# Local attention in groups of two row steps

## The reference

```
def local_attention(q, k, v):            # (b, heads, n, 64)
    bq = q.reshape(b, h, w, WINDOW, d) * QK_SCALE          # WINDOW = 128
    bk, bv = look_around(bk), look_around(bv)              # the window before and its own
    sim = einsum('bhwid,bhwjd->bhwij', bq, bk)
    mask = (i < j) | (i > j + WINDOW) | (j == -1)
    attn = softmax(where(mask, -max, sim))
    return einsum('bhwij,bhwjd->bhwid', attn, bv)
```

## Time and profile before

| | |
|---|---|
| median of 3 runs | 7475.08 us |
| lowest and highest | 7471.83 and 7477.56 us |
| profiled execution: time, span | 7471.83 us, 7471.8 us |
| mean granted clock of TensorE | 0.921 |
| busy: PE, DVE, ACT, POOL | 83%, 63%, 37%, 18% of the span |
| first and last score product of the four stages | 1310.7 to 1529.7, 2135.5 to 2353.6, 6043.2 to 6262.9, 6871.9 to 7090.5 us |

### The profile page before, as it was taken

How to read it: one execution, slowest core, us unless ns; L and a number is a source line. 1 busy time by engine, 2 the same in 40 slices (tenths; PEclk the granted TensorE clock), 3 DMA queues, 4 the chain that set the end, 5 groups by cost and what they waited for, 6 DMA issues and landing times. The chain is left out here.

```text
span 7471.8 us, 109245 instructions
## 1 busy us (share of the span) xinstructions
PE 6232.5 (83%) x31152; PEld 3226.2 (43%) x31152; DVE 4699.7 (63%) x11759; ACT 2751.9 (37%) x6050; POOL 1321.0 (18%) x1051
## 2 busy tenths in 40 slices
PE   5788859989988886999974588987995888998979
PEld 2333334655456442222223353344553456544655
DVE  4666557734665545999967649984336764357735
ACT  0155514722354210666651105541110364224711
POOL 1211106100431002000000005530003531025100
PEclk9899979989999997999996699998998999999989
DMA  5433244652456435333314221124212456235541
GB/s 165 129 72 69 62 129 145 190 188 81 130 164 196 143 101 174 80 80 83 87 50 118 81 82 40 37 73 112 73 50 90 142 165 196 72 94 154 174 151 54
DMA packets 946481, 836.62 MB, mean 112 GB/s; under 512 B 240872, under 2 KB 801984, under 8 KB 945728
## 3 DMA queue, kind: packets, MB, share of 16 engines
q1 hardware_dynamic: 498352, 507.29, 23.5%
q10 hardware_dynamic: 425472, 304.20, 13.1%
q0 software_dynamic: 22144, 18.99, 0.8%
HBM read 506.25 MB, written 346.03 MB: 114 GB/s over the span
## 5 line engine op out<-in xcount | busy, mean ns | idle before, releaser
L1395 ACT ACTIVATE Catt_E<-Catt_t 128x512 f32<-128x512 f32 x1024 | 579.1, 596 | 321.1 <-DVE Catt_t L1358 246.8
L1344 DVE CUSTOM_DVE_ANT_0 Catt_S<-Catt_s,Catt_win 128x1024 f32<-128x1024 f32 x512 | 621.5, 1215 | 4.9 <-DMA Catt_win<-skewed 3.2
L1344 DVE CUSTOM_DVE_ANT_0 Aatt_S<-Aatt_s,Aatt_win 128x128 f32<-128x128 f32 (+7 forms) x512 | 379.2, 757 | 233.7 <-PE Aatt_s L1271 206.6
L1395 ACT ACTIVATE Aatt_E<-Aatt_t 128x512 f32<-128x512 f32 (+3 forms) x768 | 341.3, 491 | 251.3 <-PE Aatt_t L1303 201.8
L1300 PE MATMUL Catt_t<-Catt_Q,Catt_K 123*128 123x512 bf16 x1024 | 364.8, 388 | 46.9 <-ACT Catt_E L1395 19.6
L1271 PE MATMUL Catt_s<-Catt_K,Catt_Q 96*128 96x512 bf16 x1024 | 322.9, 398 | 22.3 <-DMA Catt_K<-k_parts 12.1
L1358 DVE TENSOR_TENSOR Catt_t<-Catt_t,Catt_near 128x256 f32<-128x256 f32 (+2 forms) x640 | 284.8, 457 | 85.7 <-PE Catt_t L1300 77.4
L1322 PE MATMUL Catt_o<-Catt_E,Catt_V 128*32 128x256 f32 x4096 | 327.0, 391 | 0.0
L2362 PE MATMUL scan_cum<-scan_X,scan_upto 128*128 128x512 f32 x512 | 264.7, 607 | 25.4 <-DVE scan_X L2431 23.7
L2360 PE MATMUL scan_cum<-scan_X,scan_after 128*128 128x512 f32 x448 | 240.6, 619 | 40.9 <-DVE scan_pi L2442 40.9
L1322 PE MATMUL Aatt_o<-Aatt_E,Aatt_V 128*32 128x256 f32 (+1 forms) x2816 | 222.9, 361 | 41.7 <-ACT Aatt_O L1403 41.6
(11 more groups left out here) (723 smaller groups left out, 14232.4 us busy)
## 6 DMA issues: line engine op xcount, KB each, us to landing
moe_cb<-c_s SPq DMA_DIRECT2D x16, 1024.0 KB
skewed<-lines POOLq DMA_DIRECT2D x8, 1920.0 KB, 12.8
Catt_win<-skewed SPq DMA_DIRECT2D x16, 960.0 KB, 4.7
rec<-state_in_r ACTq DMA_DIRECT2D x32, 416.0 KB
scan_r<-rec SPq DMA_DIRECT2D x64, 208.0 KB, 2.5
Aatt_Q<-q_parts SPq DMA_DIRECT2D x32, 384.0 KB, 4.3
Aatt_K<-k_parts SPq DMA_DIRECT2D x32, 384.0 KB, 5.6
Catt_Q<-q_parts SPq DMA_DIRECT2D x32, 384.0 KB, 4.3
```

What stands on the lines that cost most here:

```text
L1344: v.tensor_tensor_reduce(out=S[:, j % 2, 0:w], in0=s_ps[j % 2][:, 0:w], in1=win[:, 0 if causal else h, w0:w0 + w], scale=-1.0, scalar=BIG, ...
L1395: a.activation(E[:, kb % NB, h, lo:hi], bank(it, n)[:, 0:hi - lo], ACT.Exp, scale=scale).then_inc(exped, 1)
```

## The change

Row steps go by groups of two: group i is steps 2i and 2i+1. TensorE does, at position i, the scores of group i (four products with one wait before them and one semaphore increment behind the last), the turns of group i-2, the values of group i-3, and `turn_sums` last. One bank `s_ps[i % 2][h]` holds both steps' scores of head h, in its first and its second half. VectorE waits once for all scores of a group, then does its four masks; its copies have a lag of two groups. ScalarE does `move_o` (lag 4) first, then the exponentials of the first step, the copy, and those of the second. The rings S, E and `nmax` have 8 slots instead of 4, and the counts of the semaphores follow.

```diff
@@ -769,8 +769,9 @@
 
 def stage_local_attention(nc, name, q_s, k_s, v_s, r_s, oT_s, scale):
 
-    PAIRS, hd, R, PT_R = 4, 64, 4, 4
+    PAIRS, hd, R, PT_R = 4, 64, 8, 4
     ST = B * NT
+    TWOS = ST // 2
     keys = [(max(u - 1, 0), u + 1) for u in range(NT)]
     kn = [keys[j % NT][1] - keys[j % NT][0] for j in range(ST)]
     window = LocalWindow()
@@ -867,16 +868,20 @@
             t.sem_inc(r_turned, 2)
             t.wait_ge(ident_made, 1)
 
-            def scores(it, j):
-                b, u, n = j // NT, j % NT, it * ST + j
-                if u == 0:
+            def scores(it, i):
+                b, n = 2 * i // NT, it * TWOS + i
+                if 2 * i % NT == 0:
                     t.wait_ge(head_in[b], it * 32 + 32)
-                t.wait_ge(masked, 2 * n + 2)
-                k0, w = keys[u][0] * P, kn[j] * P
-                for h in range(2):
-                    f = slice(h * hd, (h + 1) * hd)
-                    t.matmul(s_ps[j % 2][h][:, 0:w], qk[f, b, 0, u * P:(u + 1) * P], qk[f, b, 1, k0:k0 + w],
-                             start=True, stop=True).then_inc(s_done, 1)
+                t.wait_ge(masked, 4 * n + 4)
+                for e in range(2):
+                    j = 2 * i + e
+                    u, w = j % NT, kn[j] * P
+                    k0 = keys[u][0] * P
+                    for h in range(2):
+                        f = slice(h * hd, (h + 1) * hd)
+                        ins = t.matmul(s_ps[i % 2][h][:, e * 2 * P:e * 2 * P + w], qk[f, b, 0, u * P:(u + 1) * P], qk[f, b, 1, k0:k0 + w],
+                                       start=True, stop=True)
+                ins.then_inc(s_done, 1)
 
             def turn(it, j):
                 n = it * ST + j
@@ -904,8 +909,9 @@
                                        PT[:, j % PT_R, c:c + P], start=kb == 0, stop=kb == kn[j] - 1)
                 ins.then_inc(pv_done, 1)
 
-            def turn_sums(it, j):
-
+            def turn_sums(it, i):
+
+                j = 2 * i + 1
                 if j % NT < NT - 1:
                     return
                 b = j // NT
@@ -913,28 +919,35 @@
                 moved(t, it, j - 1)
                 t.transpose(pt[0][0:2 * NT, 0:P], rinv[:, b % 2, :], ident[:]).then_inc(r_turned, 1)
 
-            written_out(t, PAIRS, ST, ((0, scores), (5, values), (3, turn), (3, turn_sums)))
+            def both(step):
+
+                return lambda it, i: (step(it, 2 * i), step(it, 2 * i + 1))
+
+            written_out(t, PAIRS, TWOS, ((0, scores), (2, both(turn)), (3, both(values)), (2, turn_sums)))
 
         @block.vector
         def _(v):
-            v.sem_inc(masked, 4)
+            v.sem_inc(masked, 8)
             v.sem_inc(pt_moved_v, 2)
             v.sem_inc(inverted, 2)
             v.sem_inc(r_moved, 1)
             v.sem_inc(r_out, 32)
             v.wait_ge(win_made, 1)
 
-            def mask(it, j):
-                n, w, w0 = it * ST + j, kn[j] * P, window.start(j % NT)
-                for h in range(2):
-                    v.wait_ge(s_done, 2 * n + (h + 1))
-                    v.wait_ge(exped, 2 * n + (h + 1))
-                    apart(v, pl.dve_unread)
-                    v.tensor_tensor_reduce(out=S[:, j % R, h, 0:w], in0=s_ps[j % 2][h][:, 0:w], in1=win[:, w0:w0 + w],
-                                           scale=-scale, scalar=BIG, op0=ALU.add, op1=ALU.min,
-                                           accum_out=nmax[:, j % R, h:h + 1]).then_inc(masked, 1)
-
-            def invert(it, j):
+            def mask(it, i):
+                v.wait_ge(s_done, it * TWOS + (i + 1))
+                for e in range(2):
+                    j = 2 * i + e
+                    n, w, w0 = it * ST + j, kn[j] * P, window.start(j % NT)
+                    for h in range(2):
+                        v.wait_ge(exped, 2 * n + (h + 1))
+                        apart(v, pl.dve_unread)
+                        v.tensor_tensor_reduce(out=S[:, j % R, h, 0:w], in0=s_ps[i % 2][h][:, e * 2 * P:e * 2 * P + w], in1=win[:, w0:w0 + w],
+                                               scale=-scale, scalar=BIG, op0=ALU.add, op1=ALU.min,
+                                               accum_out=nmax[:, j % R, h:h + 1]).then_inc(masked, 1)
+
+            def invert(it, i):
+                j = 2 * i + 1
                 if j % NT < NT - 1:
                     return
                 b = j // NT
@@ -942,11 +955,13 @@
                 v.wait_ge(r_turned, it * B + (b + 1))
                 v.reciprocal(rinv[:, b % 2, :], rsum[:, b % 2].rearrange("p h u -> p (h u)")).then_inc(inverted, 1)
 
-            def move(it, j):
-                if not by_act(j):
-                    move_pt(v, v.tensor_copy, it, j, pt_moved_v)
-
-            def move_sums(it, j):
+            def move(it, i):
+                for j in (2 * i, 2 * i + 1):
+                    if not by_act(j):
+                        move_pt(v, v.tensor_copy, it, j, pt_moved_v)
+
+            def move_sums(it, i):
+                j = 2 * i + 1
                 if j % NT < NT - 1:
                     return
                 b = j // NT
@@ -954,7 +969,7 @@
                 v.wait_ge(r_out, it * (B * 16) + (b + 1) * 16)
                 v.tensor_copy(R16[:, b % 2, :], pt[0][0:2 * NT, 0:P]).then_inc(r_moved, 1)
 
-            written_out(v, PAIRS, ST, ((0, mask), (1, invert), (3, move), (3, move_sums)))
+            written_out(v, PAIRS, TWOS, ((0, mask), (1, invert), (2, move), (2, move_sums)))
 
         @block.scalar
         def _(a):
@@ -964,21 +979,24 @@
                 a.sem_inc(o_out[i], 16)
 
             def exp(it, j):
+
                 n, w = it * ST + j, kn[j] * P
                 b, u = j // NT, j % NT
                 a.wait_ge(pt_done, n + 1)
                 if u == 0:
                     a.wait_ge(inverted, it * B + (b + 1))
                 for h in range(2):
-                    a.wait_ge(masked, 2 * n + (h + 5))
+                    a.wait_ge(masked, 2 * n + (h + 9))
                     a.activation(E[:, j % R, h, 0:w], S[:, j % R, h, 0:w], ACT.Exp, bias=nmax[:, j % R, h:h + 1],
                                  scale=-1.0, accum_out=rsum[:, b % 2, h, u:u + 1]).then_inc(exped, 1)
 
-            def move(it, j):
+            def move(it, i):
+                j = 2 * i + 1
                 if by_act(j):
                     move_pt(a, lambda out, in_: a.activation(out, in_, ACT.Copy), it, j, pt_moved_a)
 
-            def move_o(it, j):
+            def move_o(it, i):
+                j = 2 * i + 1
                 if j % 4 < 3:
                     return
                 b, half, n = j // NT, j // 4 % 2, it * ST + j
@@ -987,7 +1005,8 @@
                     a.wait_ge(o_out[b], it * 16 + 16)
                 a.activation(OT[:, b, half * CH:(half + 1) * CH], o_ps[half][:], ACT.Copy).then_inc(o_moved, 1)
 
-            written_out(a, PAIRS, ST, ((0, exp), (3, move), (6, move_o)))
+            first, second = (lambda it, i: exp(it, 2 * i)), (lambda it, i: exp(it, 2 * i + 1))
+            written_out(a, PAIRS, TWOS, ((4, move_o), (0, first), (2, move), (0, second)))
 
 
 def stage_local_out(nc, name, oT_s, w, out, res):
```

## The result

The changed kernel takes 7385.18 us (median of 4 runs, 7380.4 to 7387.2) against 7473.45 us for the kernel before in the same comparison (median of 4, 7462.48 to 7477.56). The ratio is 0.9882 with a 95% interval of 0.9868 to 0.9896: 88 us less, where 82 were forecast, and the time lies 8 us under the forecast 7393 us, inside the range of 7361 to 7420. The profiled execution took 7380.4 us.

A forecast was written before the change was run, and what follows sets the result against it. TensorE was taken to bound the stages, with a fixed pause at each change of shape. Per block -2.0 + 0.15 + 0.47 = -1.38 us; 14 blocks plus 1.2 give 20.5 per stage, 82 in four: 7475 - 82 = 7393 us, range 7361 to 7420.

The forecast's parts named there:

- What bounds the stage: Local attention stages: TensorE sets the pace, paying about 0.15 us once per section (0.20 for scores).
- Joined sections: TensorE's scores, turns and values of two steps in a row save 0.50 us per slot, 2.0 per block.
- Rival (b): Turns and values don't join because each step keeps its own waits; only scores do: 7463 us, chance 0.07.
- Rival (c): Nothing joins, since the pause belongs to each product group and its waits: slower, 7512 us, chance 0.05.
- The turn of the sums: On TensorE per block: 0.15 us more as its own section, 0.47 standing for VectorE's copy behind four masks.
- Other waits at nothing: Other new waits, on copies, exponentials, rings and loads, cost nothing; the copies have 0.4 us of cover or more.
- SyncE's loads: They wait for values of a block needed again three blocks later; the longer lag was put at nothing.
- VectorE's share: VectorE's busy share in the profile after was forecast at 81%; its 10.2 us per block fits the new block.
- Edges: Ends of each stage: the last interval between turns of the sums saves 1.2 us, the start 0.
- The start of a stage: Old and new wait for masks and exponentials there: 0 taken, between 1 us lost and 1 gained.
- rival (e): TensorE's clock falls to its lower level in the stages with longer stretches of turns: near 7,900 us, chance 0.02.
- Rival (d): The change does nothing because another engine holds the slot near 3.5 us: 7475 us, chance 0.03.

The follow-up runs named there:

- e2: Changed kernel, but TensorE does turns and values step by step in turns, two more changes of shape per slot: 7441.96 us, ratio 0.9954.
- e11: Changed kernel, but products with V use all 128 columns, one head after the other (output not the reference's): 7526.11 us, one run.
- e4: Changed kernel, but each step's scores of a head have their own bank and wait: 7364.94 us, ratio 0.9854.
- e1: Changed kernel, but VectorE copies the even step between the masks of the slot's first and second step: 7359.91 us, ratio 0.9842.
- e7: Changed kernel, but in groups of four steps, ring PT at 8, sums in a scores bank, VectorE's copies between masks: 7337.28 us, ratio 0.9822.

## Why the prediction was right

*What bounds the stage.* Right: TensorE, with a fixed part in each section. e2 gives the price by itself: two more changes per slot cost 0.30 us. What the rows of before alone could not tell, whether it is the shape or the kind of instruction, e11 settles for turns and values.

*Joined sections, -2.0 per block.* Right: 1.06 and 1.03 us, measured as forecast. Rival (b), that the steps' own waits would part them, is out: eight turns go through with one pause. Rival (c) with it. In e4 even the score section has a wait in its middle and keeps its length.

*The turn of the sums, +0.15 and +0.47.* Right in mechanism and place, a little high in both: 0.23 instead of 0.26 for the section, so +0.12, and 0.43 for the stand. A block lost 1.45 us (2.0 - 0.12 - 0.43) where 1.38 were forecast, which over 14 blocks in four stages is 4 us.

*Other waits at nothing.* Right but for one: turns, values and scores show no idle time beyond the pause in the steady part, except the 0.53 us for k in H1att. SyncE's loads were put at nothing with much room, and cost next to nothing with little: between 1340 and 1480 us SyncE waited 9.4 us, in 10 times, for the write of the sums before the change, and 35.8 us in 11 times after it. That hardly any of it reached TensorE is in part luck, as e1's H1att shows with a block only 0.46 us shorter. VectorE's share was forecast at 81% and is 74%: instructions in a row overlap by 0.07 to 0.1 us, and more of them stand in a row now, so a block keeps VectorE busy for 9.3 us, where the forecast took the 10.2 of before; it cost nothing.

*Edges.* The last interval saves 1.30 (1.2 forecast). Its turns stand as described; weight loads and, below, VectorE at the same time:

```profile
1500.01 0.63 PEld L908 LDWEIGHTS B0att_o<-B0att_PT,B0att_V 128*64 128x64 f32 x12 [0.17 <-issue]
1501.47 0.42 PEld L895 LDWEIGHTS B0att_pt<-B0att_ident,B0att_E 128*128 128x128 f32 x4 [0.83 <-ACT B0att_E L990]
1502.07 0.42 PEld L895 LDWEIGHTS B0att_pt<-B0att_ident,B0att_E 128*128 128x128 f32 x4 [0.18 <-ACT B0att_E L990]
```

```profile
1500.67 1.28 DVE L818 COPY B0att_PT<-B0att_pt 128x512 f32<-128x512 f32 x2
```

The row names ScalarE for the load at 1501.47, but these turns' exponentials were done before 1499.86, when those of the next group began (ScalarE in order of time); the load comes 0.1 us behind the end of VectorE's first copy (1500.67 + 0.69), the wait that really ended last. The start of a stage saves 1.2, -0.8, 0.8 and -0.5 us in the four stages, 0.2 in the mean: the 0 that was taken is right, and its bounds of 1 either way hold for the mean, though not for B0att. With 4 us from the blocks and about 1 from starts and ends, the four stages are 87 us shorter in the profiled executions where 82 were forecast. The medians differ by 88; the interval of the ratio allows about 10 us either way, so the forecast's miss of 6 in that difference is inside it.

*The clock, rival (e).* Out: 1.00 in the steady part, with longer rows of turns. What the Trainium skill says of transposes and the clock gate ("TensorE: Matmul & The Clock Gate", "PE-mode transpose"), that they don't count as busy in the same way, doesn't show in this mix.

*Rival (d).* Out: no engine but TensorE holds the slot. What came next to a limit was not VectorE but the queue of transfers, in e1's H1att and in the groups of four, which neither the prediction nor the expectation of e7 had named as one.

## What to carry to other kernels

Compare sections of the same kind and different length in the trace: if the time is a fixed part plus so much per instruction, the fixed part is what grouping saves, and an instruction of the same shape that already follows without a gap speaks for it before anything is built. When work is grouped, look for the one small instruction that waits for something inside its own group; here a different order on the engine that it waits for (the copy between the masks) gave another 25 us with no more work. When a stage gets faster, read the queue of transfers next, in every stage and not only in one, and look for a small write that gates later loads and is issued behind big ones; moving it to another engine's queue gave 32 us here, though it stayed slow.

## What the runs showed of the hardware

- A change of the array's tile costs TensorE about 0.15 us (0.20 with the score products), seen as idle time of the weight loads: 0.12 to 0.17 us behind 128 columns and 0.33 us behind 256. It doesn't depend on waits, on the engine waited for, or on whether a section holds transposes or products. The Trainium skill, "TensorEngine Tiling (Array Packing)", "Key Properties", says that changing the tiling mode drains the engine. e11 agrees: with the same tile for turns and values the pause between them is gone (0.83 us instead of 1.03). A transpose with 16 columns behind one with 128 pays nothing: its load starts where the fourth load ends, and it takes 0.11 us.
- A write of 8 KB issued right behind 1.5 MB of loads on one queue was 7.2 us away from the step that it gates, and 10.2 us with a store of 512 KB more in front. From another engine's queue, 1.0 us behind the end of the last load's issue, it was still 6.0 us. At 8 to 10 us behind the loads, in B0att of the kernel before, it was 1.5 to 1.7 us.
- Behind a wait of 2.83 us TensorE's granted clock was 0.50 from 6970 to 6973 us (e1, H1att), and turns of two steps took 1.57 us there instead of 1.03.
- The named releaser of a wait for several semaphores can be one that was done long before (ScalarE at 1501.47, where VectorE ended it).
